# Scale and shift of normalised rows in a graph kernel: operands of 96 array rows against operands of 64 rows in two halves

## What is computed

```
cond  = silu(emb @ f_w1 + f_b1) @ f_w2 + f_b2              # 1250 x 16
def cond_layer_norm(x, cond, sw, sb, bw, bb):              # sw, bw: 16 x 512
    xn = (x - mean(x)) * rsqrt(var(x) + EPS)
    return xn * (1.0 + cond @ sw + sb) + cond @ bw + bb
for i in range(4):
    x = x + attention(cond_layer_norm(x, cond, s1_w[i], s1_b[i], b1_w[i], b1_b[i]))
    y = cond_layer_norm(x, cond, s2_w[i], s2_b[i], b2_w[i], b2_b[i])
    x = x + relu(y @ m_w1[i] + m_b1[i]) @ m_w2[i] + m_b2[i]
```

## Time and profile before

| what | value |
|---|---|
| three runs | 1797.63, 1799.87 and 1801.14 us, median 1799.87 us |
| the profiled execution | 1802.24 us, span of its instructions 1800.5 us |
| PE matmul busy | 1751.8 us, 97% of the span, 11706 matmuls |
| weight loads busy | 1497.9 us, 83% |
| DVE, ACT, POOL busy | 68%, 43%, 31% |
| granted TensorE clock | 0.993 of full on average |

### The profile page before, as it was taken

How to read it: one execution, slowest core, us unless ns; L and a number is a source line. 1 busy time by engine, 2 the same in 40 slices (tenths; PEclk the granted TensorE clock), 3 DMA queues, 4 the chain that set the end, 5 groups by cost and what they waited for, 6 DMA issues and landing times.

```text
span 1800.5 us, 31833 instructions
## 1 busy us (share of the span) xinstructions
PE 1751.8 (97%) x11706; PEld 1497.9 (83%) x11706; DVE 1232.1 (68%) x2182; ACT 771.4 (43%) x1270; POOL 559.0 (31%) x878
## 2 busy tenths in 40 slices
PE   6999999999999999999999999999999999999998
PEld 5997554688999888889998888799988887999877
DVE  5998546636777668367776683577767835777676
ACT  4553220124666442246664412366644213666431
POOL 1000721402333634023335440133345401233383
PEclk9999999999999999999999999999999999999999
DMA  4002200221110222111112131201121222111221
GB/s 126 1 1 103 100 29 36 102 82 44 45 59 31 86 63 81 68 55 31 62 45 80 41 110 39 84 30 60 45 83 40 66 83 73 39 45 60 61 94 69
DMA packets 62793, 110.47 MB, mean 61 GB/s; under 512 B 14680, under 2 KB 24920, under 8 KB 62656
## 3 DMA queue, kind: packets, MB, share of 16 engines
q1 hardware_dynamic: 62656, 108.64, 18.6%
HBM read 86.62 MB, written 22.00 MB: 60 GB/s over the span
## 4 chain that ended last, share of the span: by engine, by line
PE 90%; DVE 5%; issue 2%; DVEq 1%; ACT 1%; DMA 1%; POOL 0%; SPq 0%; POOLq 0%; ACTq 0%
PE ps L1420 52%; PE ps L1453 14%; PE ps L1537 6%; PE ps L1486 4%; PE ps L1410 4%; PE ps L1353 3%; PE ps L1379 2%; PE ps L1479 2%; PE ps L1492 2%; DVE masked_s L1129 1%; DVE hot L979 1%; DMA x<-in_x_dram 1%; DVE pT L1113 1%; DVE hot L982 0%; DVEq L979 0%
## 5 line engine op out<-in xcount | busy, mean ns | idle before, releaser
L1113 DVE TENSOR_TENSOR pT<-ps,pT 128x640 fp32r<-128x640 f32 (+1 forms) x320 | 243.9, 804 | 154.7 <-ACT pT L894 154.7
L1420 PE MATMUL ps<-yT,w 128*128 128x512 f32 (+1 forms) x1728 | 330.1, 352 | 0.0
L1420 PE MATMUL ps<-kh,q_parts 128*128 128x512 f32 (+3 forms) x1440 | 315.9, 363 | 10.2 <-DVE small L1129 7.0
L1420 PEld LDWEIGHTS ps<-yT,w 128*128 128x128 f32 x1728 | 280.6, 189 | 45.0
L894 ACT CAST pT<-ps 128x640 fp32r<-128x640 f32 (+1 forms) x320 | 202.3, 684 | 253.1 <-PE ps L1537 242.6
L1420 PEld LDWEIGHTS ps<-kh,q_parts 128*128 128x128 f32 (+1 forms) x1440 | 243.9, 185 | 58.2 <-issue 6.0
L1420 PE MATMUL ps<-w,kh 128*128 128x512 f32 (+1 forms) x960 | 238.9, 400 | 7.9 <-DVE x L1228 4.4
L1420 PEld LDWEIGHTS ps<-w,kh 128*128 128x128 f32 (+1 forms) x960 | 176.6, 188 | 48.0 <-DVE x L1228 5.2
L834 ACT ACTIVATE s<-masked_s,small 128x1280 f32 (+1 forms) x156 | 215.1, 1379 | 0.0
L1453 PE MATMUL ps<-pT,v 128*128 128x256 f32 (+1 forms) x1600 | 214.2, 280 | 0.0
L1453 PEld LDWEIGHTS ps<-pT,v 128*128 128x128 f32 x1600 | 199.5, 190 | 0.0
(11 more groups left out here) (171 smaller groups left out, 2440.5 us busy)
## 6 DMA issues: line engine op xcount, KB each, us to landing
mask<-mask_dram SPq DMA_DIRECT2D x24, 640.0 KB, 5.1
x_spill<-x SPq DMA_DIRECT2D x36, 256.0 KB
x<-x_spill SPq DMA_DIRECT2D x36, 256.0 KB, 4.5
rep<-rec_dram SPq DMA_DIRECT2D x64, 128.0 KB, 3.2
w_raw<-in_L_gnn_m_w_dram SPq DMA_DIRECT2D x8, 1024.0 KB, 6.3
mask_y<-mask_dram SPq DMA_DIRECT2D x12, 640.0 KB, 5.3
mask_dram<-mask_out SPq DMA_DIRECT2D x10, 640.0 KB, 2.9
w_l<-in_L_gnn_W_dram SPq DMA_DIRECT2D x2, 2048.0 KB, 10.8
```

The source lines that it names most:

```text
L1113: nc.vector.tensor_tensor(pT[:, 1, places, k * P:k * P + R], turn_bank(half, R), pT[:, 0, places, k * P:k * P + R].bitcast(F32), ALU.subtr ...
L1420: mine = mm(to, left(a), right(b), start=first and n == 0, stop=final and n == 2)
```

## The change

The scale's operands go into rows 0 to 63 and the shift's into rows 64 to 127, so `film` is [128, 512] and `cond` [128, 1250]. Within a half the rows are 0 to 15 high by high, 16 the bias, 17 the one of the scale, 18 the low part of the bias, 32 to 47 the low part of `cond` by the high part of `film`, 48 to 63 the high part of `cond` by the low part of `film`. `FS` multiplies the first 64 rows and `FB` the last 64; their order among PE's jobs stays. POOL makes `film` by two operations on 128x512, of which the first multiplies by a column of zeros and ones (`low_rows`). A norm's load is 10 transfers. `C2` now has a stationary operand of 16 rows by 128 columns (`f_second`, `f_w2` six times), DVE writes 128 rows in one go and splits them by two operations. `f_second`, a bias column and `low_rows` are filled by DVE and POOL at the start, and 12 small transfers of `f_w2` and `f_b2` take the place of two, behind a wait of SP for DVE's fills. The diff, without the lines around it and without declarations of semaphores:

```
@@ -241 @@
+        low_rows = sb("low_rows", [P, 2])
-        f_bias = sb("f_bias", [16, 2])
+        f_bias = sb("f_bias", [P, 2])
@@ -260 @@
-        cond = at("cond", 0, "cond", [96, N], F32R)
+        cond = at("cond", 0, "cond", [P, N], F32R)
@@ -298 @@
-        film = at("film", 0, "film", [96, 2 * D], F32R)
-        film_raw = at("film_raw", 0, "film_raw_t", [96, 2 * D])
+        film = at("film", 0, "film", [P, D], F32R)
+        film_raw = at("film_raw", 0, "film_raw_t", [P, D])
@@ -334 @@
-        f_mats = at("q_parts", 0, "f_mats", [64, 32])
+        f_mats = at("q_parts", 0, "f_mats", [64, 16])
+        f_second = at("q_parts", 512, "f_second", [16, P])
+        cond_raw = at("v", 15360, "cond_raw", [P, N])
@@ -393 @@
+        FILM_ROWS, FILM_BIAS, FILM_ONE = (0, 32, 48), (16, 18), 17
@@ -410 @@
-            sp.dma_start(f_mats[0:16, 16:32], f_w2[:, :]).then_inc(small_in, 16)
-            sp.dma_start(f_bias[:, 0:1], f_b1.rearrange("(p o) -> p o", o=1)).then_inc(small_in, 16)
-            sp.dma_start(f_bias[:, 1:2], f_b2.rearrange("(p o) -> p o", o=1)).then_inc(small_in, 16)
+            sp.dma_start(f_bias[0:16, 0:1], f_b1.rearrange("(p o) -> p o", o=1)).then_inc(small_in, 16)
@@ -428 @@
-                    for r in range(3):
-                        sp.dma_start(film_raw[32 * r:32 * r + 16, c * D:(c + 1) * D], wt[i]).then_inc(film_in, 16)
-                        sp.dma_start(film_raw[32 * r + 16:32 * r + 17, c * D:(c + 1) * D], bt[bass.ds(i, 1)]).then_inc(film_in, 16)
+                    for r in FILM_ROWS:
+                        sp.dma_start(film_raw[64 * c + r:64 * c + r + 16, :], wt[i]).then_inc(film_in, 16)
+                    for r in FILM_BIAS:
+                        sp.dma_start(film_raw[64 * c + r:64 * c + r + 1, :], bt[bass.ds(i, 1)]).then_inc(film_in, 16)
@@ -441 @@
+            sp.wait_ge(cond_clear, 2)
+            for c in range(2):
+                for r in FILM_ROWS:
+                    sp.dma_start(f_second[:, 64 * c + r:64 * c + r + 16], f_w2[:, :]).then_inc(second_in, 16)
+                    sp.dma_start(f_bias[64 * c + r:64 * c + r + 16, 1:2], f_b2.rearrange("(p o) -> p o", o=1)).then_inc(second_in, 16)
@@ -595 @@
-                pool.wait_ge(film_in, (n + 1) * 12 * 16)
+                pool.wait_ge(film_in, (n + 1) * 2 * (len(FILM_ROWS) + len(FILM_BIAS)) * 16)
-                nc.gpsimd.tensor_copy(film[:], film_raw[:]).then_inc(film_hi, 1)
+                nc.gpsimd.tensor_tensor(film[:], film_raw[:], low_rows[:, 0:1].broadcast_to([P, D]), ALU.mult).then_inc(film_hi, 1)
-                nc.gpsimd.tensor_tensor(film[64:96, :], film_raw[64:96, :], film[64:96, :].bitcast(F32),
-                                        ALU.subtract).then_inc(film_ready, 1)
+                nc.gpsimd.tensor_tensor(film[:], film_raw[:], film[:].bitcast(F32), ALU.subtract).then_inc(film_ready, 1)
-            nc.gpsimd.affine_select(out=film_raw[0:32, 0:D], in_=film_raw[0:32, 0:D], compare_op=ALU.not_equal, fill=1.0,
-                                    base=-17, pattern=[[0, D]], channel_multiplier=1).then_inc(padded, 1)
+            nc.gpsimd.affine_select(out=film_raw[0:32, :], in_=film_raw[0:32, :], compare_op=ALU.not_equal, fill=1.0,
+                                    base=-FILM_ONE, pattern=[[0, D]], channel_multiplier=1).then_inc(padded, 1)
+            pool.wait_ge(padded, 2)
+            for n, (rows_of, value) in enumerate((((0, P), 0.0), ((32, 64), 1.0), ((32, 48), 0.0), ((96, P), 1.0), ((96, 112), 0.0))):
+                if n:
+                    pool.wait_ge(low_made, n)
+                nc.gpsimd.memset(low_rows[rows_of[0]:rows_of[1], 0:1], value).then_inc(low_made, 1)
+            for n, row in enumerate((FILM_BIAS[1], 64 + FILM_BIAS[1])):
+                pool.wait_ge(low_made, 5 + n)
+                nc.gpsimd.affine_select(out=low_rows[:, 0:1], in_=low_rows[:, 0:1], compare_op=ALU.not_equal, fill=1.0,
+                                        base=-row, pattern=[[0, 1]], channel_multiplier=1).then_inc(low_made, 1)
+            pool.wait_ge(low_made, 7)
@@ -920 @@
+            nc.vector.memset(f_second[:], 0.0).then_inc(cond_clear, 1)
+            chain(nc.vector.memset(f_bias[:, 1:2], 1.0))
+            dve.sem_inc(cond_clear, 1)
+            for (r0, r1), value in (((0, P), 0.0), ((32, 48), 1.0), ((96, 112), 1.0)):
+                chain(nc.vector.memset(low_rows[r0:r1, 1:2], value))
@@ -966 @@
-            dve.wait_ge(small_in, 16 * 6)
+            dve.wait_ge(small_in, 16 * 4)
@@ -1050 @@
-                chain(nc.vector.memset(emb[0:32, 3, :], 1.0))
-                nc.vector.tensor_copy(cond[0:32, :], emb[0:32, 3, :]).then_inc(cond_dve, 1)
+                nc.vector.tensor_scalar(cond[:], cond_raw[:], low_rows[:, 1:2], None, ALU.mult).then_inc(cond_dve, 1)
-                nc.vector.tensor_copy(cond[64:96, :], emb[0:32, 3, :]).then_inc(cond_dve, 1)
-                nc.vector.tensor_tensor(cond[32:64, :], emb[0:32, 3, :], cond[0:32, :].bitcast(F32),
-                                        ALU.subtract).then_inc(cond_dve, 1)
+                nc.vector.tensor_tensor(cond[:], cond_raw[:], cond[:].bitcast(F32), ALU.subtract).then_inc(cond_dve, 2)
@@ -1078 @@
-                    nc.vector.tensor_scalar(emb[0:16, 0, c0:c0 + cn], bank[0:16, 0:cn], f_bias[:, 0:1], None,
+                    nc.vector.tensor_scalar(emb[0:16, 0, c0:c0 + cn], bank[0:16, 0:cn], f_bias[0:16, 0:1], None,
-                    nc.vector.tensor_scalar(emb[0:16, 3, c0:c0 + cn], bank[0:16, 0:cn], f_bias[:, 1:2], None,
+                    dve.wait_ge(second_in, 16 * 4 * len(FILM_ROWS))
+                    nc.vector.tensor_scalar(cond_raw[:, c0:c0 + cn], bank[:, 0:cn], f_bias[:, 1:2], None,
@@ -1394 @@
-                    pe.wait_ge(small_in, 16 * 6)
+                    pe.wait_ge(small_in, 16 * 4)
+                    pe.wait_ge(second_in, 16 * 4 * len(FILM_ROWS))
-                    mine = mm(bank[0:16, 0:cn], f_mats[0:16, 16:32], emb[0:16, 2, c0:c0 + cn], start=True, stop=True)
+                    mine = mm(bank[:, 0:cn], f_second[:], emb[0:16, 2, c0:c0 + cn], start=True, stop=True)
@@ -1475 @@
-                        c0 = 0 if kind == "FS" else D
-                        mine = mm(bank[0:R, :], cond[:, a * P:a * P + R], film[:, c0:c0 + D], start=True, stop=True)
+                        half = slice(0, 64) if kind == "FS" else slice(64, P)
+                        mine = mm(bank[0:R, :], cond[half, a * P:a * P + R], film[half, :], start=True, stop=True)
```

More of the change, by code:

```diff
@@ L342, in gnn_kernel @@
         idx_in, x_in_s, small_in, noise_in = sem("idx_in"), sem("x_loaded"), sem("small_in"), sem("noise_in")
+        second_in, cond_clear = sem("second_in"), sem("cond_tiles_clear")
         w1_in, w2_in, b2_in = sem("w1_in"), sem("w2_in"), sem("b2_in")
@@ L359, in gnn_kernel @@
         mask_in = [sem(f"mask_in_{n}") for n in range(4)]
-        padded, tails_clear = sem("padding_cleared"), sem("tails_clear")
+        padded, tails_clear, low_made = sem("padding_cleared"), sem("tails_clear"), sem("low_rows_made")
         w_in = [sem("w_in_first"), sem("w_in_second")]
```

## The result

The changed kernel takes 1808.45 us (median of six runs, 1807.03 to 1810.16) against 1797.77 us for the kernel before, also six runs. The two medians lie 10.7 us apart; the ratio over all runs is 1.0051 [1.0041, 1.0061], or 9.2 us more (7.4 to 11.0). The same kernel was timed again later (`e5_again`): 1808.81 against 1797.58, ratio 1.0064 [1.0050, 1.0078]. Slower was forecast, at 1811.9 us. The profiled execution took 1809.33 us, its span 1807.6.

A forecast was written before the change was run, and what follows sets the result against it. PE, without gaps around the pairs, was taken as the bound: 68 unhidden pairs at 0.175 us more give 11.9, plus 0.1 for other edits, 12.0 on 1799.87, so 1811.9 us; range 1803 to 1829.

The forecast's parts named there:

- The wait of a switch: On PE at each change between 128-row and 64-row matmuls, into and out of a pair: 0.09 us of wait.
- the cheap switch: Rival, at the pairs: 64-row weights still load ahead; 1797.1 us with waits alone, 1782.8 with none; chance 0.16.
- The load of the scale: At the start of each pair: the scale's weight load is no longer hidden and takes 0.105 us.
- The stagger s: Within a pair: the shift's matmul starts 0.02 us behind the scale's, taken from C1's loads.
- the second load behind the first: Rival, within a pair: the second load waits for the whole first, s = 0.105; 17.8 us more, 1817.7 us; chance 0.15.
- The load on the way out: Behind each pair: the next job's weight load is exposed, 0.105 us.
- What is hidden: In the four WO stages: PE's 1.10 us wait for DVE covers three pairs' delay, 0.53 us; 12 pairs of 80.
- No overlap: Rival, within a pair: the shift starts when the scale has streamed, s = 0.235; 26.9 us more, 1826.8 us; chance 0.13.
- The other edits: C2's wider load, POOL's split, transfers and fills at the start: 0.1 us more in all, the rest hidden.
- L1479's share of the chain: Profile sign: the scale and shift matmuls' share of the chain, 2% before, should rise.
- 0.645: Timeline sign: the next job's first matmul should come about 0.645 us behind the pair's first.

The follow-up runs named there:

- e5_again: Changed kernel, unaltered, timed again; 1808.81 us against 1797.58 for the kernel before, ratio 1.0064.
- e2_samehalf: Changed kernel with scale and shift both in rows 0 to 63 (film 64x1024), so the pair cannot overlap; 1824.47 us, ratio 1.0145 to the kernel before.
- e1_rows128: Changed kernel with all its edits, but pair matmuls read all 128 rows, zeros in film's other half (128x1024); 1798.74 us, ratio 0.9997 to the kernel before.
- the control: Kernel before, with PE's order altered so that its 96-row pairs stand two by two; 1799.01 us, ratio 1.0004 to the kernel before.
- e6_turn_first: Changed kernel with the transposes T moved ahead of their pair on PE in 64 places; 1814.56 us, ratio 1.0096 to the kernel before.
- e8_before_1: Kernel before, unaltered, one further profiled execution to compare what lies outside the stages; mean granted clock 0.994.
- e10_before_2: Kernel before, unaltered, another single profiled execution for the same comparison; 1797.46 us, two falls of the granted clock.

## Why the prediction was right, and which terms were off

**Direction, range and size** were right: +12.0 us was forecast on the median of the runs, 9.2 (7.4 to 11.0) and 11.5 (9.0 to 14.0) were measured. But the stages hold 7.5 of the 11.9 us that were put there, and outside them lie some 2.3 that were not in the sum: 1.0 at equal clock, the rest by falls of the clock. Part of the closeness is luck.

**The wait of a switch**, 0.09 us: right. The pair starts 0.318 behind the product in place of 0.228; 0.32 was forecast. Full columns make no difference, and the cheap switch, which hung on C1's narrow columns, is out. By "TensorEngine Tiling (Array Packing)" in the Trainium skill, section Tiling Modes, changing the mode drains TensorE; the trace agrees, with 0.09 us of nothing.

**The load of the scale**, 0.105: right. The distance from the pair to the next job, 0.43, has to hold this load, one stream and the second wait: 0.105 + 0.235 + 0.09 = 0.430.

**The stagger s** was the first term off: 0.004 us in place of 0.02. The two loads lie within 0.19 us, so neither waits for the other, and the second load behind the first (+17.8 us) falls. I took s from the loads of C1, which has both matmuls in one half. The section Part 3 of "TensorE: Matmul & The Clock Gate" in the Trainium skill has 4 ns between the starts of packed tiles; the trace agrees, and the sum by it would have been 1.1 us nearer.

**The load on the way out** was the larger one: 0.105 was counted behind every pair, but `T` stands behind most pairs and exposes 0.055. I had taken the price from the earlier trace rows, where a product is next. With both corrections, a pair costs 0.430 + 0.09 + 0.105 - 0.47 = 0.155 ahead of a product (measured 0.153) and, with 0.055 in place of the second 0.105, 0.105 ahead of `T` (measured 0.094), where 0.175 was forecast for all. The M2 tile took 3.77 in place of 3.85.

**What is hidden**: the place and the mechanism were right (WO stages only, behind DVE), the size follows the smaller price: 0.25 to 0.3 us a stage in place of 0.53.

**No overlap** (+26.9) falls by `e2_samehalf`, which is what it describes: 15.9 us in the stages above the kernel after.

**The other edits** cost nothing in the stages, as forecast; `e1_rows128` shows it. Outside them the 1.0 us at equal clock may be theirs; no run tells.

**Two statements on the profile were wrong.** L1479's share of the chain was to rise; it is 2% before and after. The pair's piece of a tile fell, 0.47 to 0.42, since the records put the wait ahead of the pair on the product and the way out on `T`. And 0.645 us from the pair's first matmul to the next job's was a slip: that figure includes the wait ahead of the pair and the load of the next job. By my own terms the distance is 0.45, measured 0.43.

## What to carry to other kernels

Packing two short matmuls into the two halves of the array saves one stream (0.23 us at 512 columns here) and costs a visit to another mode: a wait of 0.09 us each way, the load of the first weights (0.105) and the exposed load of what comes next (0.055 to 0.105), 0.34 to 0.39 us in all. By this sum it pays only where one visit holds several such pairs, and then only if their banks are free: here, with two pairs a visit, packing gave back 2.2 us against the control and the order cost 3.2, mostly in waits for DVE, so the two together did not beat the kernel before. Zeros in the unused rows cost no time on TensorE, so where the depth fits into 128 rows there is no need to leave the mode; what the wider operand costs the engine that makes it has to be counted too, as in `e1_rows128`. And where falls of the clock move the time by some microseconds, a stage that is cut out of the trace tells a change of 1 us that the total cannot.

## What the runs showed of the hardware beyond what was expected

- Going back to fp32 transposes exposes half the load that going back to a product does (0.055 against 0.105 us); `e6_turn_first` shows that it goes with the job behind the switch. Why is open.
- A pair of 128 rows is no dearer than one of 96: 0.46 against 0.47 us to the next job, 0.9 us less in the stages.
- What PE does alone repeats within 0.06 us over some 420 us of stages, while the same kernel's time varies by 3 to 5 us. Between `e8_before_1` and `e10_before_2` the falls of the granted clock account for it (mean 0.994 against 0.997, 3.4 us in what lies behind the start of the edge counts); between the first execution of the kernel before and `e8_before_1` it is what lies ahead of them (2.1 us).
- The granted clock falls to the level of 1.2 GHz behind waits of PE as short as 2.2 us, and of two or three of 0.7 to 1.0 us close together (in `e2_samehalf` at the start of an attention), in some executions and not in others.
